# Places of the expert results computed by VectorE for four tiles at once

## The chip, the cores and the metric

The kernel runs on one core of a Trainium2 chip. The metric is device time in microseconds of one launch. TensorE (PE) multiplies, VectorE (DVE), ScalarE (ACT) and GpSimd (POOL) compute, SyncE (SP) issues most transfers, and engines meet only by semaphores.

## The reference

One block of a model on 16 x 512 tokens of width 128, in float32: a modulated layer norm, a linear recurrence (the mixer), then a second modulated layer norm and a mixture of experts, 2 of 8 per token. Cut to what matters here:

```python
logits = xt @ Wr + br
p = softmax(logits)
probs, idx = top_k(p, 2)
probs = probs / probs.sum(axis=-1, keepdims=True)
h = einsum('td,edf->etf', xt, W1) + b1[:, None, :]
h = layernorm(relu(h), g1, be1)
y = einsum('etf,efd->etd', h, W2) + b2[:, None, :]
y = layernorm(relu(y), g2, be2)
gate = (one_hot(idx, 8) * probs[..., None]).sum(axis=1)
out = einsum('te,etd->td', gate, y)
x = x + gb * out
```

## The kernel before

The mixer stage runs over the 16 batches. It writes each token's normalised row twice, into the regions of its two experts in a buffer in device memory (`rows_d`), as a row of ROW = 130 numbers: TOKEN (the number of the result, 2 x token), EXPERT (the token's first expert) and 128 values (H). From about 166 us the expert stage runs over EXPERT_TILES = 135 tiles of 128 such rows; each tile has one expert.

For tile i the work goes so. SyncE loads its rows into `hrow[i % 8]`. TensorE turns them (L1651, step i - 2), ScalarE and VectorE split them into a high and a low part (L821, L1221), TensorE makes the 512 hidden values (L1668 to L1670, step i), ScalarE takes the positive part (L825), VectorE their statistics (L1226, L1484). TensorE turns the hidden values (L1676) and multiplies by W2 (L1686, step i + 4) into one single bank, which VectorE empties in step i + 5 (L1455). There follow ScalarE (L949), statistics (L1474, L1479), a scaling (L1466, step i + 7), and the last scaling and shift, for some tiles on VectorE (L1447), else on ScalarE (L957) and GpSimd (L720). GpSimd stores the 128 result rows with an indirect transfer (L732), whose places are `target[i % 32]`.

These places are the matter here: place = TOKEN + (EXPERT is not the tile's expert). VectorE computes them in `target_of` (L1434 to L1439), one operation per tile at the end of step i:

```python
vec.tensor_scalar(target[i % TARGETS][:], hrow[n][:, EXPERT], tile_e[:, i:i + 1],
                  hrow[n][:, TOKEN], ALU.not_equal, ALU.add).then_inc(target_ready, 1)
```

It waits for the tile's rows and, since `target` has 32 buffers, for the result store 32 tiles back. Who waits for `target_ready`: SyncE in `load_next(i)` (L573 to L580), before it loads rows into the slot of tile i - 8; behind this wait in its queue stand the row load and `load_shifts(i - 6)` (L571), which itself waits until a shift buffer is free. And GpSimd in `store_results` (L722).

The order on each engine is written out by hand: `run_tiles` calls one `expert_step(s)` per step and engine. From step 53 on VectorE also combines the two results of finished tokens (`early_sum`, L1550) in 44 pieces at the end of a step, GpSimd multiplies and adds them (L773, L779), ScalarE scales (L922). In the first 13 steps VectorE makes the second table of tiles between the others (`round2_table`). `tile_e` holds the expert of each tile, on all partitions. GpSimd also writes the last of the mixer's rows (L704), up to step 43. SLOTS is 8.

## Time and profile before

| | |
|---|---|
| median of 3 runs | 505.99 us (504.31 to 506.33) |
| profiled execution | 503.4 us, its span 501.6 us |
| busy over the span | PE 475.5, DVE 452.2, ACT 406.3, POOL 348.3 us |
| operations of VectorE | 2245 |
| transfers | 78.36 MB, mean 156 GB/s |

Busy time counts overlapping operations once. Matmuls are pipelined, so a busy TensorE is not yet at its best rate; the spacing of starts tells more. In a timeline the first number is the start in us from the span's start, the second the duration; the bracket, where there is one, is the idle time before and what ended it. On VectorE an operation may start while the one before it is finishing, so that durations add up to more than the time. "tile" and "step" below count from 0; step s is where TensorE makes the hidden values of tile s.

### The profile page before, as it was taken

How to read it: one execution, taken by the hardware profiler on the slowest of the kernel's cores; microseconds unless marked ns; L12 is line 12 of the kernel's file. 1: busy time of each engine (PE TensorE's matmuls, PEld its weight loads, DVE VectorE, ACT ScalarE, POOL GpSimd, SP SyncE). 2: the span in 40 equal slices, each digit the busy share in tenths (PEclk: the TensorE clock that was granted, in tenths of full speed). 3: DMA queues.
4: the chain of work that ended last, by engine and by line, in shares of the span. 5: the costliest groups of instructions: out<-in, count | busy, mean ns of one | idle time of the engine just before them, and what ended most of it. 6: DMA issues, size and time to landing. Idle time of an engine off the chain costs nothing. (4 is left out here: it accounts for less than half of the span.)

```text
span 501.6 us, 15039 instructions
## 1 busy us (share of the span) xinstructions
PE 475.5 (95%) x3083; PEld 366.6 (73%) x3083; DVE 452.2 (90%) x2245; ACT 406.3 (81%) x1118; POOL 348.3 (69%) x461
## 2 busy tenths in 40 slices
PE   7998999999999899999999999999999999999994
PEld 6454555555567688888888888888888888888851
DVE  6879999998888899899998899999999999999994
ACT  3678898988865777777887888989998889989883
POOL 1003666666767777788888878888887888888871
PEclk9999999999999999999999999999999999999998
DMA  5990511114211578988726986766667667667555
GB/s 165 313 256 18 132 50 48 43 56 106 64 43 56 136 172 163 166 246 205 192 82 160 200 221 137 204 192 185 202 183 178 186 191 207 166 181 212 189 177 167
DMA packets 80364, 78.36 MB, mean 156 GB/s; under 512 B 11433, under 2 KB 73052, under 8 KB 80276
## 3 DMA queue, kind: packets, MB, share of 16 engines
q1 hardware_dynamic: 71860, 60.48, 48.9%
q0 software_dynamic: 8416, 16.93, 9.5%
q8 instruction: 29, 0.48, 0.4%
q14 instruction: 59, 0.48, 0.4%
HBM read 55.20 MB, written 22.62 MB: 155 GB/s over the span
## 5 line engine op out<-in xcount | busy, mean ns | idle before, releaser
L704 POOL DMA_INDIRECT expert_rows<-rows_ring,slot x128 | 123.4, 964 | 93.2 <-issue 74.7
L732 POOL DMA_INDIRECT expert_results<-y,target x119 | 120.4, 1012 | 32.7 <-issue 28.1
L1686 PE MATMUL bank<-W,h2T 128*128 x720 | 96.4, 277 | 1.8 <-DVE wmod L1455 0.9
L1686 PEld LDWEIGHTS bank<-W,h2T 128*128 128x128 f32 x720 | 87.5, 191 | 12.5 <-issue 5.6
L1668 PE MATMUL bank<-W1hi,h3hi 128*128 x135 | 65.5, 485 | 1.3 <-DVE h3lo L1221 1.3
L949 ACT ACTIVATE v<-wmod 128x128 f32<-128x128 f32 x135 | 41.8, 310 | 29.3 <-DVE vg L1466 25.5
L1226 DVE BATCH_NORM_STATS2 stf<-h1T 128x6 f32<-128x512 f32 x90 | 59.2, 658 | 0.0
L814 ACT ACTIVATE n<-X,nm,rs 128x128 f32<-128x128 f32 x128 | 52.7, 488 | 7.1 <-DVE nm L1395 7.1
L961 ACT ACTIVATE sde<-mve,eps 128x2 f32<-128x2 f32 (+1 forms) x138 | 40.6, 295 | 17.9 <-DVE mve L1479 15.6
L1676 PE MATMUL bank<-ident_wr,h1T 128*128 128x128 f32 x360 | 54.4, 274 | 0.2 <-ACT third_rT L829 0.2
L829 ACT ACTIVATE h2T<-bank 128x512 f32<-128x512 f32 x90 | 52.7, 586 | 1.0 <-PE bank L1676 0.9
L1669 PE MATMUL bank<-W1lo,h3hi 128*128 x135 | 53.4, 396 | 0.0
L1670 PE MATMUL bank<-W1hi,h3lo 128*128 x135 | 53.3, 395 | 0.0
L825 ACT ACTIVATE h1T<-bank 128x512 f32<-128x512 f32 x90 | 53.0, 589 | 0.0
L1455 DVE SCALAR_TENSOR_TENSOR wmod<-bank,rse,shifts 128x128 f32<-128x128 f32 x119 | 40.8, 343 | 13.2 <-PE bank L1686 11.9
L1686 PE MATMUL bank<-W,third_rT 128*128 x360 | 48.2, 277 | 1.1 <-DVE wmod L1455 0.9
L1686 PEld LDWEIGHTS bank<-W,third_rT 128*128 128x128 f32 x360 | 43.7, 192 | 6.3 <-issue 2.8
L1466 DVE SCALAR_TENSOR_TENSOR vg<-v,mve,shifts 128x128 f32<-128x128 f32 x119 | 44.7, 376 | 0.0
L1676 PEld LDWEIGHTS bank<-ident_wr,h1T 128*128 128x128 f32 x360 | 41.7, 141 | 1.5 <-issue 0.5
L1221 DVE TENSOR_TENSOR h3lo<-bank,h3hi 128x128 fp32r<-128x128 f32 x135 | 37.9, 281 | 0.5 <-ACT h3hi L821 0.3
L1474 DVE BATCH_NORM_STATS2 sty<-v 128x6 f32<-128x128 f32 x135 | 37.9, 281 | 0.2
L1651 PE MATMUL bank<-ident_wr,hrow 128*128 128x128 f32 x135 | 36.2, 272 | 0.0
(253 smaller groups left out, 1172.0 us busy)
## 6 DMA issues: line engine op xcount, KB each, us to landing
shifts<-expert_shifts SPq DMA_DIRECT2D x119, 192.0 KB
hrow<-expert_rows SPq DMA_DIRECT2D x135, 65.0 KB
xi<-expert_results SPq DMA_DIRECT2D x12, 512.0 KB, 6.0
out_x<-X SPq DMA_DIRECT2D x15, 256.0 KB, 3.9
X<-in_L_attn_x SPq DMA_DIRECT2D x7, 512.0 KB, 7.4
b_ring<-b_two_parts SPq DMA_DIRECT2D x135, 4.0 KB
W1lo<-in_L_ffn_W SPq DMA_DIRECT2D x4, 512.0 KB, 5.9
expert_rows<-rows_ring,slot POOLq DMA_INDIRECT x128
```

The source lines that it names most:

```text
L704: nc.gpsimd.indirect_dma_start(out=rows_d, out_offset=bass.IndirectOffsetOnAxis(ap=slot[q][:, n // TOPK, n % TOPK:n % TOPK + 1], axis=0), ...
L732: nc.gpsimd.indirect_dma_start(out=results_d, out_offset=bass.IndirectOffsetOnAxis(ap=target[i % TARGETS][:], axis=0), in_=y[k], in_offset ...
L814: ins = nc.scalar.activation(dst[:, j:j + 1, :], X[:, bass.ds(b * J + j, 1), :], ACT.Identity, bias=nm_[:, x_tiles + j:x_tiles + j + 1], s ...
L825: nc.scalar.activation(r[i % DEPTH], hidden_bank(i)[:], ACT.Relu).then_inc(r_ready, 1)
L829: nc.scalar.activation(rT[i % DEPTH], turned_bank[:], ACT.Copy).then_inc(rT_ready, 1)
L1226: vec.bn_stats(stf[i % 2][:], r[i % DEPTH]).then_inc(stf_ready, 1)
L1466: vec.scalar_tensor_tensor(wide(vg[p][:]), wide(v[p][:]), mve[p][:, 1, 0:1], wide(shift_rows[ring(s - 7)][:, D:2 * D]), ALU.subtract, ALU. ...
L1668: mm(h, h3hi[i % DEPTH], W1hi[:, bass.ds(e, 1), :], start=False, stop=False)
L1669: mm(h, h3hi[i % DEPTH], W1lo[:, bass.ds(e, 1), :], start=False, stop=False)
L1670: mm(h, h3lo[i % DEPTH], W1hi[:, bass.ds(e, 1), :], start=False, stop=True).then_inc(h_done, 1)
L1676: ins = tr(turned_bank[:, ch * P:(ch + 1) * P], r[i % DEPTH][:, ch * P:(ch + 1) * P], ident[:])
L1686: ins = mm(acc, rT[i % DEPTH][:, ch * P:(ch + 1) * P], W2[:, bass.ds(e * CF + ch, 1), :], start=(ch == 0), stop=(ch == CF - 1))
```

## The change

The eight row slots become one tensor with the slots side by side, and the 32 columns of targets another. In every fourth step (1, 5, 9, ...) VectorE compares the EXPERT column of four slots with four columns of `tile_e` (`other_experts_of`), and after one operation more adds the four TOKEN columns (`targets_of`). The second waits for the first by a new semaphore. Tiles 4k to 4k + 3 are done in step 4k + 1. The semaphore `target_ready` then rises by four at once. The last group has three tiles.

```diff
-        hrow = [sb(f"hrow_{n}", [P, ROW])[:] for n in range(SLOTS)]
+        hrow_ring = sb("hrow_ring", [P, SLOTS, ROW])
+        hrow = [hrow_ring[:, n, :] for n in range(SLOTS)]
...
-        target = [sb(f"target_{n}", [P, 1], I32) for n in range(TARGETS)]
+        targets = sb("targets", [P, TARGETS], I32)
+        target = [targets[:, n:n + 1] for n in range(TARGETS)]
+        TARGETS_AT_ONCE = 4
+        other_expert = sb("other_expert", [P, TARGETS_AT_ONCE])
...
-            def target_of(i, n):
-                dve.wait_ge(hrow_loaded[n], (i + SLOTS - n) * (16 // SLOTS))
+            def other_experts_of(i):
+                count = min(TARGETS_AT_ONCE, EXPERT_TILES - i)
+                for m in range(i, i + count):
+                    dve.wait_ge(hrow_loaded[m % SLOTS], (m + SLOTS - m % SLOTS) * (16 // SLOTS))
+                expert = hrow_ring[:, i % SLOTS:i % SLOTS + count, EXPERT].rearrange("p n o -> p (n o)")
+                vec.tensor_tensor(other_expert[:, 0:count], expert, tile_e[:, i:i + count], ALU.not_equal).then_inc(other_expert_ready, 1)
+
+            def targets_of(i):
+                count = min(TARGETS_AT_ONCE, EXPERT_TILES - i)
+                dve.wait_ge(other_expert_ready, i // TARGETS_AT_ONCE + 1)
                 if i >= TARGETS:
-                    dve.wait_ge(results_stored[(i - TARGETS) % RESULTS], result_count(i - TARGETS))
-                vec.tensor_scalar(target[i % TARGETS][:], hrow[n][:, EXPERT], tile_e[:, i:i + 1],
-                                  hrow[n][:, TOKEN], ALU.not_equal, ALU.add).then_inc(target_ready, 1)
+                    for m in range(i - TARGETS, i - TARGETS + count):
+                        dve.wait_ge(results_stored[m % RESULTS], result_count(m))
+                token = hrow_ring[:, i % SLOTS:i % SLOTS + count, TOKEN].rearrange("p n o -> p (n o)")
+                vec.tensor_tensor(targets[:, i % TARGETS:i % TARGETS + count], other_expert[:, 0:count], token,
+                                  ALU.add).then_inc(target_ready, count)
...
+                if s % TARGETS_AT_ONCE == 1:
+                    other_experts_of(s - 1)
                 if on(s - 6, EXPERT_TILES):
                     ins = value_norm(s, q)
...
-                if on(s, EXPERT_TILES):
-                    target_of(s, n % SLOTS)
+                if s % TARGETS_AT_ONCE == 1:
+                    targets_of(s - 1)
```

On VectorE, at the end of step 61 and in step 62, there stands before (L1479 ends the statistics of the values, L1550 is a combining piece, L1455 empties the value bank):

```order
L1226 BN_STATS stf<-decay 128x6 [waits r_ready]
L1479 BN_AGGR mve<-sty 128x2 [waits sty_ready]
L1438 TENSOR_SCALAR target<-hrow,tile_e 128x1 [waits result_stored5,hrow_loaded5]
L1550 SCALAR_TENSOR_TENSOR n_1<-xi,gate,n_1 128x128 [waits early_y0g_ready]
L1455 SCALAR_TENSOR_TENSOR wmod<-bank,rse,shifts 128x128 [waits rse_ready,shifts_loaded1,y_done]
...
L1226 BN_STATS stf<-h1T 128x6 [waits r_ready]
L1479 BN_AGGR mve<-sty 128x2 [waits sty_ready]
L1438 TENSOR_SCALAR target<-hrow,tile_e 128x1 [waits result_stored6,hrow_loaded6]
L1455 SCALAR_TENSOR_TENSOR wmod<-bank,rse,shifts 128x128 [waits rse_ready,shifts_loaded2,y_done]
```

And in the changed kernel, where the same lines have other numbers (L1494, L1567, L1470; L1444 and L1453 are the pair):

```order
L1231 BN_STATS stf<-decay 128x6 [waits r_ready]
L1444 TENSOR_TENSOR other_expert<-hrow_ring,tile_e 128x4 [waits hrow_loaded6,hrow_loaded7,hrow_loaded5,hrow_loaded4]
L1494 BN_AGGR mve<-sty 128x2 [waits sty_ready]
L1453 TENSOR_TENSOR targets<-other_expert,hrow_ring 128x4 [waits result_stored5,result_stored6,result_stored4,result_stored7,other_expert_ready]
L1567 SCALAR_TENSOR_TENSOR n_1<-xi,gate,n_1 128x128 [waits early_y0g_ready]
L1470 SCALAR_TENSOR_TENSOR wmod<-bank,rse,shifts 128x128 [waits rse_ready,shifts_loaded1,y_done]
...
L1231 BN_STATS stf<-h1T 128x6 [waits r_ready]
L1494 BN_AGGR mve<-sty 128x2 [waits sty_ready]
L1470 SCALAR_TENSOR_TENSOR wmod<-bank,rse,shifts 128x128 [waits rse_ready,shifts_loaded2,y_done]
```

The operation at the end of each step is gone, and one of the pair stands on each side of the value statistics in step 61.

On VectorE in steps 0 to 4, between the making of the second table, there stands before:

```order
L1120 CAST cnt_i<-bank 128x8 [waits count_done,table_ready]
L1438 TENSOR_SCALAR target<-hrow,tile_e 128x1 [waits hrow_loaded0]
L1126 TENSOR_SCALAR cnt<-cnt_i 128x56 [waits counts_ready]
L1438 TENSOR_SCALAR target<-hrow,tile_e 128x1 [waits hrow_loaded1]
L1128 CAST nt_i<-cnt 128x56 [waits table_step]
L1438 TENSOR_SCALAR target<-hrow,tile_e 128x1 [waits hrow_loaded2]
L1484 BN_AGGR mve<-stf 128x2 [waits stf_ready]
L1130 TENSOR_SCALAR nt_i<-nt_i 128x56 [waits table_step]
L1438 TENSOR_SCALAR target<-hrow,tile_e 128x1 [waits hrow_loaded3]
L1463 RECIPROCAL rse<-sde 128x1 [waits sde_ready]
L1221 TENSOR_TENSOR h3lo<-bank,h3hi 128x128 [waits h3hi_ready]
```

and in the changed kernel:

```order
L1125 CAST cnt_i<-bank 128x8 [waits count_done,table_ready]
L1444 TENSOR_TENSOR other_expert<-hrow_ring,tile_e 128x4 [waits hrow_loaded2,hrow_loaded3,hrow_loaded1,hrow_loaded0]
L1131 TENSOR_SCALAR cnt<-cnt_i 128x56 [waits counts_ready]
L1453 TENSOR_TENSOR targets<-other_expert,hrow_ring 128x4 [waits other_expert_ready]
L1133 CAST nt_i<-cnt 128x56 [waits table_step]
L1499 BN_AGGR mve<-stf 128x2 [waits stf_ready]
L1135 TENSOR_SCALAR nt_i<-nt_i 128x56 [waits table_step]
L1478 RECIPROCAL rse<-sde 128x1 [waits sde_ready]
L1226 TENSOR_TENSOR h3lo<-bank,h3hi 128x128 [waits h3hi_ready]
```

Of four operations two are left before the low part of tile 5 (h3lo).

## Rows read from the trace of the kernel before

**Rows 1.** Busy by stretch: length, then PE, PEld, DVE, ACT, POOL (x), clock, DMA

```profile
292.00:468.00 176.00, 175.73 (x1286) 152.34 (x1285) 166.01 (x718) 158.85 (x494) 145.65 (x227) 1.00 0.70 191
```

**Rows 2.** Timeline of TensorE, first hidden matmul of tiles 56, 124, 132: start us, us

```profile
290.81 0.50 PE L1668 MATMUL bank<-W1hi,h3hi 128*128 x1
...
449.80 0.51 PE L1668 MATMUL bank<-W1hi,h3hi 128*128 x1
...
468.18 0.50 PE L1668 MATMUL bank<-W1hi,h3hi 128*128 x1
```

**Rows 3.** Timeline of TensorE: start us, us, operation, [idle before <-releaser]

```profile
168.34 0.49 PE L1668 MATMUL bank<-W1hi,h3hi 128*128 x1 [1.26 <-DVE h3lo L1221]
...
269.47 0.14 PEld L1651 LDWEIGHTS bank<-ident_wr,hrow 128*128 128x128 f32 x1 [0.39 <-DMA hrow<-expert_rows]
...
302.94 0.27 PE L1651 MATMUL bank<-ident_wr,hrow 128*128 128x128 f32 x1
303.05 1.05 PE L1686 MATMUL bank<-W,h2T 128*128 x8
...
305.08 0.27 PE L1651 MATMUL bank<-ident_wr,hrow 128*128 128x128 f32 x1
305.27 1.15 PE L1686 MATMUL bank<-W,h2T 128*128 x8
...
431.80 0.27 PE L1651 MATMUL bank<-ident_wr,hrow 128*128 128x128 f32 x1
432.22 1.15 PE L1686 MATMUL bank<-W,h2T 128*128 x8 [0.15 <-issue]
```

**Rows 4.** Timeline of VectorE, steps 60 to 62 and the end of step 115

```profile
301.01 0.28 DVE L1474 BATCH_NORM_STATS2 sty<-v 128x6 f32<-128x128 f32 x1
...
301.39 0.18 DVE L1479 BATCH_NORM_AGGREGATE mve<-sty 128x2 f32<-128x6 f32 x1
...
302.00 0.35 DVE L1455 SCALAR_TENSOR_TENSOR wmod<-bank,rse,shifts 128x128 f32<-128x128 f32 x1 [0.23 <-PE bank L1686]
...
303.65 0.17 DVE L1479 BATCH_NORM_AGGREGATE mve<-sty 128x2 f32<-128x6 f32 x1
303.73 0.24 DVE L1438 TENSOR_SCALAR target<-hrow,tile_e 128x1 int32<-128x1 f32 x1
303.89 0.86 DVE L1550 SCALAR_TENSOR_TENSOR n<-xi,gate,n 128x128 f32<-128x128 f32 x1
304.68 0.34 DVE L1455 SCALAR_TENSOR_TENSOR wmod<-bank,rse,shifts 128x128 f32<-128x128 f32 x1
...
430.19 0.85 DVE L1550 SCALAR_TENSOR_TENSOR n<-xi,gate,n 128x128 f32<-128x128 f32 x1
```

**Rows 5.** VectorE, single lines: count, then ns min/median/max

```profile
L1438 DVE TENSOR_SCALAR target<-hrow,tile_e x135: 232/242/274, 166.5 to 473.9; 128x1 int32<-128x1 f32 x135
...
L1466 DVE SCALAR_TENSOR_TENSOR vg<-v,mve,shifts x119: 322/332/621, 173.6 to 484.4; 128x128 f32<-128x128 f32 x119
...
L1550 DVE SCALAR_TENSOR_TENSOR n<-xi,gate,n x44: 337/381/948, 287.6 to 485.3; 128x128 f32<-128x128 f32 x44
```

**Rows 6.** Waits: engine, line, releaser: us in total, times, longest us

```profile
ACT v L949 <- DVE vg L1466: 25.5, 51, 1.1
...
SPq L571 <- POOL y L720: 42.8, 34, 9.3
...
SPq L578 <- DVE target L1438: 12.9, 6, 8.3
```

**Rows 7.** Groups of VectorE by line: count | busy us, mean ns | idle before

```profile
L1438 DVE TENSOR_SCALAR target<-hrow,tile_e 128x1 int32<-128x1 f32 x135 | 33.6, 249 | 0.0
...
L1322 DVE TENSOR_TENSOR sq<-rs 128x8 f32<-128x8 f32 (+1 forms) x34 | 5.3, 155 | 0.3
```

**Rows 8.** Timeline of GpSimd

```profile
259.31 0.49 POOL L720 TENSOR_TENSOR y<-wmod,shifts 128x128 f32<-128x128 f32 x1
...
303.72 0.47 POOL L779 TENSOR_TENSOR X<-X,scan 128x128 f32<-128x128 f32 x1
```

1 line of the change is left out of this document (added).

## The prediction, made before the changed kernel ran

> **What bounds the kernel now.** I read the views in this order: busy time by stretch, VectorE's groups by line, the spread of single lines, the timelines of TensorE, VectorE and GpSimd side by side, and last the waits. The change touches only the expert stage, 135 tiles from about 166 us on. In its steady stretch, 292 to 468 us, TensorE shows 175.73 of 176.00 us, VectorE 166.01, ScalarE 158.85 and GpSimd 145.65, at granted clock 1.00 [rows 1]. So TensorE sets the pace and VectorE runs at 94%. How close TensorE is to its own floor is seen in the starts of its first hidden matmul of each fourth tile [rows 2]: tiles 124 to 132 take 468.18 - 449.80 = 18.38 us, 9.19 us for four, and this is the spacing of the undisturbed groups everywhere. From tile 56 (290.81) to tile 132 (468.18) there are 19 groups in 177.37 us; 19 x 9.19 = 174.61, so only 2.8 us of that stretch are above TensorE's floor. No relief of VectorE can give more than that there.
>
> Where those 2.8 us lie is seen at the value matmuls (L1686), which must wait until VectorE has emptied the one value bank (L1455). Normally they start 0.11 us after the row transposition (302.94, 303.05). In step 62 it is 0.19 us (305.08, 305.27), in step 116 0.42 us (431.80, 432.22) [rows 3]. There are four steps in this stretch where VectorE's L1455 starts so late that TensorE must wait for it, of which these are the first and the last. In each of them a combining operation L1550 of 0.80 to 0.86 us stands right before (303.89, 430.19) [rows 4]; its usual time is 0.34 to 0.4, since its spread is 337/381/948 ns [rows 5]. The rest comes through ScalarE, which waits for VectorE's L1466 51 times, 25.5 us in all [rows 6], and then hands TensorE its transposed tile late.
>
> **What the change removes.** 135 operations of 249 ns, 33.6 us [rows 7], become 34 pairs. But the 249 ns overlap the next instruction: from the start of the old operation to the next start is 303.89 - 303.73 = 0.16 us [rows 4]. So in a group of four tiles four times 0.16 = 0.64 us of VectorE's queue go.
>
> **What it adds.** Per group two TENSOR_TENSOR of 128x4. The trace has none; nearest are those of 128x8, 155 ns [rows 7]. An operation of this length lets the next one start 0.08 us later (L1479, 0.17 long, at 303.65, then 303.73) [rows 4]. The second needs the result of the first: the statistics at 301.01 take 0.28 and their dependent starts at 301.39 [rows 4], 0.10 us after the end. So the second may start 0.155 + 0.10 = 0.25 us after the first, and the L1479 put between them (0.08) is hidden in that. The pair costs 0.25 + 0.08 - 0.08 = 0.25 us, all in steps 1, 5, 9 and so on: 0.09 us more than the old operation there, 0.16 us less in each of the other three steps. A group is relieved by 0.39 us; 34 groups by 13 us. As bounds I take 0.16 us for the pair (if nothing of the dependence shows) and, from above, one operation held by GpSimd as below, 0.25 + 0.61.
>
> The additions also wait in a row for four row loads, and then for the pair's own semaphore and four old result stores. The row loads of the group's last tile are asked for two steps earlier than before. They are the same that TensorE needs for its own transposition in about that step, and the result stores are some 20 tiles old, so I cost these waits at nothing; behind them on VectorE's queue stand L1479 (whose result ScalarE waits for) and the next L1455, and if a row load is late both are.
>
> **Held by GpSimd.** The old operation takes 232/242/274 ns in all 135 cases, so nothing ever holds it. Operations with two inputs from the on-chip memory do get held: L1466 goes from 332 to 621 ns and L1550 from 337 to 948 [rows 5], and the 0.86 us one at 303.89 starts 0.17 us after GpSimd's L779 (303.72) [rows 8]. Both new operations are of that kind. In 14 of the 34 groups, as at 303.73, GpSimd starts an addition within 0.02 us of the old operation's start; the first of the pair, put 0.08 us earlier, gets in ahead of it, but the second, due about 0.17 us after the old place, falls into it. In the mild cases (most L1550 at that phase take 0.37 to 0.49) it loses 0.1 us, in the bad ones up to 0.948 - 0.337 = 0.61. I take 0.1 in half of the groups, since 381 is L1550's median. The relief is then 0.34 us a group.
>
> The Trainium skill, SBUF — State Buffer, section Who interferes with whom, says that a VectorE instruction with two SBUF inputs contends with a GpSimd instruction that reads SBUF, and that the later one is blocked for the whole of the other. By it every one of those seconds would lose what is left of GpSimd's 0.47 us. The rows agree that such operations are held, but show most of them held for less than that.
>
> **What of the relief reaches the end.** TensorE is at its floor in most groups, so there the relief becomes idle time of VectorE. Of the four late steps from 292 us on, three follow a step that loses an old operation and is not the pair's, and the wait before them shrinks by at most 0.16 us each: -0.48. Step 62 follows step 61, where the pair stands: +0.1. Through ScalarE, in the twelve or so steps (92 to 104) in which VectorE hardly idles, I put another -0.3, two removed operations. Sum: **-0.7 us**.
>
> Before 292 us there is more to gain by VectorE: TensorE waits 1.26 us for it at the start of the stage (168.34) [rows 3], and two removed operations lie ahead of this and the next such wait, worth about 0.3 us; a few stalls between 183 and 232 us give another 0.5. But I count nothing for either. GpSimd works off a backlog at its own pace there; SyncE waits up to 9.3 us, longest of its 34 waits, until GpSimd has added a shift [rows 6], which happens with the addition at 259.31 [rows 8], and the loads issued behind it are so late that TensorE waits 0.39 us for a row tile at 269.47 [rows 3]. Whoever arrives there 0.8 us earlier waits 0.8 us longer. What is late next is that load.
>
> **Moved past SyncE.** SyncE reloads a row slot only when its target is made. It waits for that 6 times, 12.9 us, of which 8.3 is the first [rows 6], ending as the stage starts. The first tile of each group is released one step (2.3 us) later than before, the last two earlier. From tile 47 on SyncE asks for tile i more than 1 us after step i-7 has ended, so the later release is not felt; in tiles 30 to 46 it is, but there the row is asked for 10 us before it is needed. Cost: nothing; without that cover up to 2.3 us per group.
>
> The profiled execution is 503.4 us (span 501.6), 2.6 below the median of 505.99; the sum gives 502.7 for it, and 505.3 for the median.
>
> **Rivals.**
> 1. *Every stall but the loads' is VectorE's lateness and goes.* Then the 2.8 us from 292 us on and 0.3 us at the start are won: 505.99 - 3.1 = 502.9. For it: the median run is 2.6 us longer than the profiled one, and may have more such stalls. Against: some stalls of about 0.3 us stand where VectorE was in time.
> 2. *GpSimd wins the port (slower).* The second of the pair, which also waits for the first, is caught by two back-to-back additions of GpSimd, as L1550 was at 303.89. In the 14 groups where the phases meet, step 1 becomes 0.25 - 0.16 + 0.61 = 0.7 us longer. TensorE has 0.45 us before it needs L1455, as its value matmuls normally start 1.05 us after it (302.00, 303.05) and where they wait 0.59 (304.68, 305.27) [rows 3, 4]. It decides when the hold exceeds about 0.36 us. Then ScalarE's share is late too, whose spare is small, and the whole 0.7 us is lost: 14 x 0.7 = 9.8, that is 515.8; if only what exceeds 0.45, 14 x 0.25 = 3.5: 509.5. I take 509.5. By the page named above this case would be more frequent than the rows make it.
> 3. *Nothing reaches the end*, or a row load that now comes in bursts of four makes good the 0.7: 506 to 507.
> 4. That the pair doesn't do what it says has no room: the order has 34 of each and none of the old.
>
> **How the numbers follow.** My case (505.3) 0.55, rival 1 (502.9) 0.18, rival 3 (506.5) 0.17, rival 2 (509.5) 0.1. A measurement of this kernel can tell about 0.5%, 2.5 us, from no change; the three runs before lie 2 us apart. Faster by over 0.5% is rival 1 and a little of mine: 0.2. Slower: rival 2, 0.1. The rest, 0.7, is same. The range takes in rivals 1 and 3 with a margin for the spread of the runs: 502.6 to 507.8.
>
> **What would show it.** VectorE's busy time falls by about 13 us or less (busy is counted once where operations overlap), the pair's operations take 0.15 to 0.2 us with a few above 0.4, the group from tile 124 to 128 still takes 9.19 us, the stretch from tile 56 to 132 becomes 176.7 us, and the row load near tile 49 still makes TensorE wait, rather longer. It is wrong if groups that took 9.19 us take more (rival 2), if tile 49's wait vanishes and the gain before 269 us is kept, or if the 2.8 us shrink below 1.

## The result

The changed kernel takes 506.96 us (median of 13 runs, 505.65 to 509.98), the kernel before, run beside it, 504.31 us (13 runs, 502.91 to 511.03). The ratio is 1.0051, 95% interval 1.0033 to 1.0070: slower by about 2.6 us, where the prediction had it faster by 0.7. The profiled execution is 507.31 us, its span 505.5 (503.4 and 501.6 before). VectorE's work did shrink: it is busy 441.6 us in place of 452.2.

### The profile page after: what moved, and what is told of

The parts are those of the page before. It is cut to its first block, busy times and chain, and to the rows that moved or that the text cites. A ratio compares the mean times of both kernels' runs of the same rounds, so it can differ in the third digit from the quotient of the medians.

```text
span 505.5 us, 15021 instructions
## 1 busy us (share of the span) xinstructions
PE 478.8 (95%) x3083; PEld 368.2 (73%) x3083; DVE 441.6 (87%) x2178; ACT 406.5 (80%) x1118; POOL 348.6 (69%) x461
## 4 chain that ended last, share of the span: by engine, by line
POOL 29%; issue 20%; POOLq 2%; DVE 1%; DMA 1%; DVEq 0%; ACT 0%; SPq 0%
POOL expert_results L737 17%; POOL y L725 4%; POOL X L784 3%; POOL scan L778 2%; POOL expert_rows L709 2%; POOLq L736 1%; DMA W<-expert_results 1%; POOLq L737 1%; DMA expert_results<-y,targets 1%; POOL xi L725 0%; POOLq L68 0%; POOLq L724 0%; DVE W L1574 0%; POOLq L735 0%; DVE W L1605 0%
## 5 line engine op out<-in xcount | busy, mean ns | idle before, releaser
L737 POOL DMA_INDIRECT expert_results<-y,targets x119 | 120.1, 1009 | 33.2 <-issue 30.6
L1703 PE MATMUL bank<-W,h2T 128*128 x720 | 97.2, 278 | 2.1 <-DVE wmod L1470 1.4
L1703 PEld LDWEIGHTS bank<-W,h2T 128*128 128x128 f32 x720 | 88.3, 193 | 13.2 <-issue 6.1
L954 ACT ACTIVATE v<-wmod 128x128 f32<-128x128 f32 x135 | 41.8, 310 | 31.1 <-DVE vg L1481 25.7
L1685 PE MATMUL bank<-W1hi,h3hi 128*128 x135 | 65.4, 484 | 1.1 <-DVE h3lo L1226 1.1
L1470 DVE SCALAR_TENSOR_TENSOR wmod<-bank,rse,shifts 128x128 f32<-128x128 f32 x119 | 40.9, 344 | 24.5 <-PE bank L1703 21.2
L1693 PE MATMUL bank<-ident_wr,h1T 128*128 128x128 f32 x360 | 55.3, 276 | 0.4 <-ACT third_rT L834 0.2
L834 ACT ACTIVATE h2T<-bank 128x512 f32<-128x512 f32 x90 | 52.9, 587 | 0.9 <-PE bank L1693 0.8
L1686 PE MATMUL bank<-W1lo,h3hi 128*128 x135 | 53.2, 394 | 0.0
L1703 PE MATMUL bank<-W,third_rT 128*128 x360 | 48.2, 277 | 1.0 <-DVE wmod L1470 0.9
L1703 PEld LDWEIGHTS bank<-W,third_rT 128*128 128x128 f32 x360 | 43.7, 191 | 6.3 <-issue 2.8
L1693 PEld LDWEIGHTS bank<-ident_wr,h1T 128*128 128x128 f32 x360 | 41.0, 142 | 2.9 <-issue 0.9
L1481 DVE SCALAR_TENSOR_TENSOR vg<-v,mve,shifts 128x128 f32<-128x128 f32 x119 | 42.7, 359 | 0.0
L1668 PE MATMUL bank<-ident_wr,hrow_ring 128*128 128x128 f32 x135 | 36.3, 273 | 0.0
```

The source lines that it names most:

```text
L737: nc.gpsimd.indirect_dma_start(out=results_d, out_offset=bass.IndirectOffsetOnAxis(ap=target[i % TARGETS][:], axis=0), in_=y[k], in_offset ...
L834: nc.scalar.activation(rT[i % DEPTH], turned_bank[:], ACT.Copy).then_inc(rT_ready, 1)
L1481: vec.scalar_tensor_tensor(wide(vg[p][:]), wide(v[p][:]), mve[p][:, 1, 0:1], wide(shift_rows[ring(s - 7)][:, D:2 * D]), ALU.subtract, ALU. ...
L1685: mm(h, h3hi[i % DEPTH], W1hi[:, bass.ds(e, 1), :], start=False, stop=False)
L1686: mm(h, h3hi[i % DEPTH], W1lo[:, bass.ds(e, 1), :], start=False, stop=False)
L1693: ins = tr(turned_bank[:, ch * P:(ch + 1) * P], r[i % DEPTH][:, ch * P:(ch + 1) * P], ident[:])
```

## The profile after

The lines of the changed kernel have moved: L1438 is now the pair L1444 and L1453, L1455 is L1470, L1466 is L1481, L1550 is L1567, TensorE's L1668, L1676 and L1686 are L1685, L1693 and L1703, ScalarE's L829 and L949 are L834 and L954, GpSimd's L720 is L725.

Busy time by stretch in the changed kernel, in the columns of [rows 1]:

```profile
292.00:468.00 176.00, 175.29 (x1265) 150.63 (x1265) 156.86 (x671) 156.63 (x484) 143.58 (x223) 1.00 0.69 186
```

VectorE is 9.15 us less busy than in [rows 1], and TensorE gets through less: 1265 recorded matmul instructions in place of 1286. The timeline of TensorE in the changed kernel, first hidden matmul of tiles 56, 124 to 128 and 132, which answers to [rows 2]:

```profile
291.76 0.50 PE L1685 MATMUL bank<-W1hi,h3hi 128*128 x1
...
452.99 0.50 PE L1685 MATMUL bank<-W1hi,h3hi 128*128 x1
...
455.15 0.48 PE L1685 MATMUL bank<-W1hi,h3hi 128*128 x1
...
457.29 0.48 PE L1685 MATMUL bank<-W1hi,h3hi 128*128 x1
...
459.53 0.48 PE L1685 MATMUL bank<-W1hi,h3hi 128*128 x1
...
462.34 0.50 PE L1685 MATMUL bank<-W1hi,h3hi 128*128 x1
...
471.71 0.50 PE L1685 MATMUL bank<-W1hi,h3hi 128*128 x1
```

The group from tile 124 to 128 takes 462.34 - 452.99 = 9.35 us, the next 9.37; before they took 9.2. From tile 56 to 132 it is 179.95 us in place of 177.37, that is 2.6 us, as much as the medians differ. The two profiled executions differ by 3.9 us: 0.9 lie ahead of tile 8 (the clock, see the last section), 0.1 from there to tile 56, these 2.6, and 0.4 behind tile 132. In the kernel before, the starts of tiles 130, 131 and 132 are:

```profile
463.30 0.48 PE L1668 MATMUL bank<-W1hi,h3hi 128*128 x1
...
465.44 0.48 PE L1668 MATMUL bank<-W1hi,h3hi 128*128 x1
```

with 468.18 in [rows 2]: 2.14 and 2.74 us. At the same places of the changed kernel's group (126, 127, 128) it is 2.24 and 2.81. So the group loses 0.10 us in the step after the pair's and 0.07 us in the next.

What VectorE does just before that is seen in its timeline. The kernel before, step 129, from one L1455 to the next:

```profile
461.00 0.35 DVE L1455 SCALAR_TENSOR_TENSOR wmod<-bank,rse,shifts 128x128 f32<-128x128 f32 x1 [0.24 <-PE bank L1686]
...
462.73 0.24 DVE L1438 TENSOR_SCALAR target<-hrow,tile_e 128x1 int32<-128x1 f32 x1
462.89 0.34 DVE L1550 SCALAR_TENSOR_TENSOR n<-xi,gate,n 128x128 f32<-128x128 f32 x1
463.15 0.34 DVE L1455 SCALAR_TENSOR_TENSOR wmod<-bank,rse,shifts 128x128 f32<-128x128 f32 x1
```

and GpSimd there:

```profile
463.00 0.56 POOL L720 TENSOR_TENSOR y<-wmod,shifts 128x128 f32<-128x128 f32 x1
```

The changed kernel, the same place of a group (step 125), VectorE:

```profile
454.99 0.35 DVE L1470 SCALAR_TENSOR_TENSOR wmod<-bank,rse,shifts 128x128 f32<-128x128 f32 x1 [0.88 <-PE bank L1703]
...
456.64 0.15 DVE L1444 TENSOR_TENSOR other_expert<-hrow_ring,tile_e 128x4 f32<-128x4 f32 x1
456.70 0.18 DVE L1494 BATCH_NORM_AGGREGATE mve<-sty 128x2 f32<-128x6 f32 x1
456.88 0.17 DVE L1453 TENSOR_TENSOR targets<-other_expert,hrow_ring 128x4 int32<-128x4 f32 x1
456.96 0.57 DVE L1567 SCALAR_TENSOR_TENSOR n<-xi,gate,n 128x128 f32<-128x128 f32 x1
457.45 0.34 DVE L1470 SCALAR_TENSOR_TENSOR wmod<-bank,rse,shifts 128x128 f32<-128x128 f32 x1
```

and GpSimd:

```profile
456.92 0.46 POOL L725 TENSOR_TENSOR y<-win,shifts 128x128 f32<-128x128 f32 x1 [0.28 <-ACT win L962]
```

Three things are to be seen. The pair costs what was forecast: the combining operation starts 1.97 us after the step's L1470 in place of 1.89. But it now starts 0.04 us behind GpSimd's addition (456.92), where it used to start 0.11 us ahead of it (463.00), and it takes 0.57 us in place of 0.34; before, it was GpSimd's addition that took 0.56 in place of 0.46. So the next L1470 comes 2.46 us after the last, in place of 2.15. And the relief of the other three steps lies in the bracket of the first row: VectorE idles 0.88 us there, until TensorE has filled the value bank. The waits say the same. Kernel before, then after:

```profile
DVE wmod L1455 <- PE bank L1686: 12.7, 49, 0.7
```

```profile
DVE wmod L1470 <- PE bank L1703: 22.1, 32, 1.1
```

VectorE waits for TensorE 9.4 us more, in fewer and longer pieces.

The rest of the way is on ScalarE and TensorE. The changed kernel, ScalarE (its relu of the values, then its copy of the turned tile), then TensorE (value matmuls, transposition of the hidden tile):

```profile
458.20 0.31 ACT L954 ACTIVATE v<-wmod 128x128 f32<-128x128 f32 x1 [0.34 <-DVE vg L1481]
458.42 0.58 ACT L834 ACTIVATE h2T<-bank 128x512 f32<-128x512 f32 x1
```

```profile
458.18 1.08 PE L1703 MATMUL bank<-W,third_rT 128*128 x8
459.14 0.63 PE L1693 MATMUL bank<-ident_wr,h1T 128*128 128x128 f32 x4
```

The copy ends at 458.42 + 0.58 = 459.00, and the transposition, which needs its buffer, starts 0.14 us later. That 0.14 is the least distance between the two in any of the traces. In the kernel before, at the same place:

```profile
464.13 0.58 ACT L829 ACTIVATE h2T<-bank 128x512 f32<-128x512 f32 x1
```

```profile
464.19 1.06 PE L1686 MATMUL bank<-W,h2T 128*128 x8
465.08 0.60 PE L1676 MATMUL bank<-ident_wr,decay 128*128 128x128 f32 x4
```

it is 465.08 - 464.71 = 0.37 us. So ScalarE's copy, which stands behind the relu, which waits for VectorE's L1481, has a spare of 0.37 - 0.14 = 0.23 us. VectorE is late by 2.46 - 2.15 = 0.31. The value matmuls themselves take that without loss: they start 0.73 us after L1470 in place of 1.04.

Of the 19 steps 1, 5, 9 ... between 292 and 468 us, 13 have a combining operation. It takes over 0.45 us in 11 of them in the changed kernel and in 1 of them before. Group by group against the kernel before, these 11 lose 1.8 us. The other two with a combining operation (steps 61 and 77) lose 0.7, and there the pair itself is late. In step 61 its second operation is the one that is held; GpSimd's additions start at 304.74 and 305.21 there:

```profile
305.01 0.67 DVE L1453 TENSOR_TENSOR targets<-other_expert,hrow_ring 128x4 int32<-128x4 f32 x1
```

In step 77 it starts 0.35 us late. Of the 6 groups without a combining operation, four have the next L1470 2.13 to 2.14 us after the last. In steps 89 and 101 the pair's second operation takes 0.45 and 0.72 us, the next L1470 comes 2.36 and 2.83 us after the last, and these two groups lose 0.2 and 0.55 us; as the other four gain nearly as much, the six together lose only 0.1. In the second pair of profiles (below) the held groups lose 0.5 us, those of steps 61, 77 and 117, in which the pair is late, 1.1, and the six 0.3. So the split between the two kinds of hold changes with the execution. The second operation of the pair over the whole kernel (min/median/max in ns):

```profile
L1453 DVE TENSOR_TENSOR targets<-other_expert,hrow_ring x34: 153/166/724, 166.8 to 475.6; 128x4 int32<-128x4 f32 x33, 128x3 int32<-128x3 f32 x1
```

## The experiments

In all tables and texts "held" is a combining operation of over 0.45 us in one of those 13 steps, and "56 to 132" the time from the first hidden matmul of tile 56 to that of tile 132, both read from the timeline of each kernel as above. "Quiet" groups are those that take 9.18 to 9.21 us in the kernel before. The stretch comes from one profiled execution: two profiles of the kernel before and the one of layout give 177.4, 177.8 and 178.4 us, so differences below about 1 us say little.

| kernel | ratio to before (95%) | 56 to 132 | held, of 13 |
|---|---|---|---|
| before (profile shown ahead) | | 177.4 us | 1 |
| changed | 1.0051 (1.0033 to 1.0070) | 180.0 | 11 |
| changed, again | 1.0049 (1.0026 to 1.0073) | 179.7 | 10 |
| layout | 0.9986 (0.9967 to 1.0005) | 178.4 | 1 |
| burst | 1.0111 (1.0080 to 1.0141) | 181.6 | 0 |
| pair0 | 0.9984 (0.9965 to 1.0002) | 178.2 | 7 |
| pair_after_sum | 1.0029 (1.0018 to 1.0041) | 179.2 | 1 |
| twos | 1.0045 (1.0030 to 1.0061) | 178.8 | 8 |
| split | 1.0040 (1.0025 to 1.0056) | 177.9 | 6 |
| pair3 | 1.0158 (1.0141 to 1.0175) | 180.8 | 10 |
| delay | 1.0048 (1.0026 to 1.0070) | 179.9 | 9 |
| delay_after | 1.0011 (0.9990 to 1.0032) | 178.5 | 1 |
| turned2 | 1.0029 (1.0006 to 1.0053) | 180.2 | 11 |
| pair0_turned | 0.9965 (0.9943 to 0.9986) | 177.1 | 10 |
| before, again | 0.9994 (0.9970 to 1.0018) | 177.8 | 1 |
| turned_only | 0.9962 (0.9943 to 0.9981) | 175.8 | 5 |
| split2 | 1.0005 (0.9983 to 1.0027) | 177.9 | 3 |
| pair0_turned, again | 0.9964 (0.9942 to 0.9986) | 176.9 | 10 |

### First set: layout, lump, place

**The changed kernel again.** No edit.

> The changed kernel once more, beside the others of this set. It tells whether the 1.2 GHz stretch of TensorE at 169 to 172 us, which only the changed kernel's trace showed and which cost it about 0.9 us at tile 8, belongs to the change. If the loss is a lump on VectorE in every fourth step (my theory), the ratio is again 1.005, groups of four tiles from 292 us on take 9.35 us instead of 9.19, whatever the clock does at 169 us. If the loss were mostly that stretch of low clock (rival), a profile without it would show a time of about 505 us and quiet groups of 9.19.

Measured 1.0049, and the quiet groups at the end are 9.36 us each. The stretch at 1.2 GHz is there again; what it is worth is settled by the kernel before again, below.

**Layout.**

```diff
-        hrow = [sb(f"hrow_{n}", [P, ROW])[:] for n in range(SLOTS)]
+        hrow_ring = sb("hrow_ring", [P, SLOTS, ROW])
+        hrow = [hrow_ring[:, n, :] for n in range(SLOTS)]
...
-        target = [sb(f"target_{n}", [P, 1], I32) for n in range(TARGETS)]
+        targets = sb("targets", [P, TARGETS], I32)
+        target = [targets[:, n:n + 1] for n in range(TARGETS)]
```

> The kernel before with the row slots in one ring tensor and the targets in one tensor, still one operation per tile; nothing else is changed. Theory (the lump in steps 1, 5, 9 ...): same time as before, ratio 1.000 within 0.001, groups of 9.19 us. Rival (where the slots and targets lie in the on-chip memory makes the loads, the transposition or VectorE's readers slower): ratio 1.005 as the whole change.

Measured 0.9986, held 1 of 13. The ring and the common tensor are not the cause.

**Burst.** Four old operations together, in the steps where the change has its pair.

```diff
-                if on(s, EXPERT_TILES):
-                    target_of(s, n % SLOTS)
+                if s % 4 == 1:
+                    for i in range(s - 1, min(s + 3, EXPERT_TILES)):
+                        target_of(i, i % SLOTS)
```

> As layout, but the four old operations of a group stand together in steps 1, 5, 9 ..., where the change has its pair. They have one on-chip tensor input and two per-partition scalars each and were never held by GpSimd. The lump is 0.64 us instead of 0.25. Theory (a lump in one step makes VectorE late there, what is freed in the other three steps becomes idle time): slower than the changed kernel, since 0.48 us are added to the step instead of 0.09 to 0.2; TensorE has about 0.45 us to spare, so at least 0.2 us a group and up to 0.5, 34 groups: ratio 1.01 to 1.03. Rival (the loss comes from the two-input operations held by GpSimd, or from the wait of the second for the first): no slower than before beyond 1.002. Rival (the loss comes from the release of row slots in bursts, which SyncE waits for): ratio 1.005 as the whole change, since the releases are the same.

Measured 1.0111, the quiet groups 9.60 us. So a lump of work in that step can cost time by itself: its +0.48 us cost a group 0.41 us. No combining operation is held here, as it starts 2.43 us after L1457, when GpSimd's addition is over. The row slots are released as in the changed kernel and the loss is more than twice as large, so the release alone doesn't set it.

**The pair one step earlier.**

```diff
-                if s % TARGETS_AT_ONCE == 1:
-                    other_experts_of(s - 1)
+                if s % TARGETS_AT_ONCE == 0:
+                    other_experts_of(s)
...
-                if s % TARGETS_AT_ONCE == 1:
-                    targets_of(s - 1)
+                if s % TARGETS_AT_ONCE == 0:
+                    targets_of(s)
```

> The changed kernel with the pair one step earlier, in steps 0, 4, 8 ..., for the tiles s to s+3 instead of s-1 to s+2. In the changed kernel VectorE idles 0.88 us before L1470 at the end of such a step. Theory: the pair fits into that idle time, step 1 is freed of it, TensorE's groups are 9.19 us again: time of before or up to 1 us below, ratio 0.998 to 1.001. Rival (the form of the operations, their hold by GpSimd or their dependence costs, wherever they stand): ratio 1.005 again. Rival (releases of row slots in bursts): 1.005 again or more, as three rows must now be there earlier.

Measured 0.9984: the loss is gone. The pair's second operation is held there far more often than in the changed kernel (over 0.4 us in 12 of 34 cases in place of 4). VectorE's timeline at the end of step 128:

```profile
462.40 0.59 DVE L1453 TENSOR_TENSOR targets<-other_expert,hrow_ring 128x4 int32<-128x4 f32 x1
463.22 0.35 DVE L1470 SCALAR_TENSOR_TENSOR wmod<-bank,rse,shifts 128x128 f32<-128x128 f32 x1 [0.22 <-PE bank L1703]
```

It takes 0.59 us and costs nothing, since L1470 still waits 0.22 us for TensorE. The combining operation of step 1 is held in 7 of 13 steps too, but it starts 0.17 us earlier than before the change (1.72 us after L1470), and the next L1470 still comes only 2.11 to 2.14 us after the last in six of the seven. In five groups VectorE waits 0.78 to 1.32 us for a row load. Neither the kind of the operations nor this early wait for four rows is the cause; the place is.

### Second set: which part of step 1

**The second operation behind the combining one.**

```diff
-                if s % TARGETS_AT_ONCE == 1:
-                    targets_of(s - 1)
                 for b, j in pieces_at(s - 1):
                     early_sum(b, j)
+                if s % TARGETS_AT_ONCE == 1:
+                    targets_of(s - 1)
```

> The changed kernel, but in steps 1, 5, 9 ... the second operation of the pair comes after the combining operation L1567 instead of before it. In the changed kernel L1567 starts at 456.96, 0.04 us after GpSimd's addition at 456.92, and takes 0.57 us, where in the kernel before it took 0.34. If this hold is what makes VectorE late (part of my theory), L1567 is 0.34 us again in quiet groups, and TensorE's groups shrink from 9.35 to 9.20 us: ratio to before 1.000 to 1.002. If the length of the pair itself is enough (rival), the groups stay at 9.3 or more: ratio 1.005. If the second operation is now the one that is held, for 0.2 us or more, the same 1.005.

Measured 1.0029, groups of 9.33 us. VectorE and GpSimd in step 125 of this kernel:

```profile
455.37 0.32 DVE L1567 SCALAR_TENSOR_TENSOR n<-xi,gate,n 128x128 f32<-128x128 f32 x1
455.60 0.44 DVE L1453 TENSOR_TENSOR targets<-other_expert,hrow_ring 128x4 int32<-128x4 f32 x1
455.97 0.34 DVE L1470 SCALAR_TENSOR_TENSOR wmod<-bank,rse,shifts 128x128 f32<-128x128 f32 x1
```

```profile
455.49 0.53 POOL L725 TENSOR_TENSOR y<-win,shifts 128x128 f32<-128x128 f32 x1 [0.29 <-ACT win L962]
```

The combining operation is ahead of the addition again and takes 0.32 us, and the small one behind it is the one held, 0.44 in place of 0.17. The next L1470 comes 2.40 us after the last, 0.25 later than before the change. Half of my first expectation was wrong: taking the hold from L1567 only hands it on to the next operation with two inputs.

**Two at a time.** Layout, with two old operations in each odd step.

```diff
-                if on(s, EXPERT_TILES):
-                    target_of(s, n % SLOTS)
+                if s % 2 == 1:
+                    for i in range(s - 1, min(s + 1, EXPERT_TILES)):
+                        target_of(i, i % SLOTS)
+                elif s == EXPERT_TILES - 1:
+                    target_of(s, s % SLOTS)
```

> Old operations, two together in each odd step, none in the even steps (ring and targets as in the layout run). A lump of +0.16 us with operations that GpSimd never holds. In the burst run +0.48 us cost TensorE 0.40 us a group. If TensorE has no spare at all in such a step (theory), +0.16 costs 0.1 to 0.16 us in steps 1, 5, 9 ... and nearly as much in steps 3, 7, 11 ...: groups of 9.3 to 9.5 us, ratio 1.004 to 1.009. If a step has 0.1 us or more to spare (rival), the quiet groups stay at 9.19 to 9.22: ratio 0.999 to 1.001, and the changed kernel's loss needs the hold of L1567 or the wait of the second operation besides.

Measured 1.0045, at the lower end of what was expected. But the reason is not the 0.16 us alone. The combining operation starts 2.07 us after L1457, where GpSimd's addition starts too (mostly from 0.03 us later to 0.15 earlier), and is held in 8 of 13 steps. This run has both cases side by side. In steps 65, 69, 121 and 125 it is not held, the next L1457 comes 2.32 or 2.33 us after the last, and the groups take 9.23 to 9.25 us. (The fifth that is not held, step 129, has 2.32 and a group of 9.52: TensorE's weight load starts 0.43 us late at 464.78, released by nothing that the profile shows, as in the second profile of the kernel before at 464.71, 0.33 us.) The eight held ones have 2.45 to 2.81 us and groups of 9.41 to 9.77. So 0.18 us of lateness cost a group about 0.05 us, and the hold on top of it the rest. In five of the 6 steps without a combining operation the next start is 2.13 or 2.14 us after the last.

The twos profile is no guide to the ratio: it took 504.42 us, the fastest of its six runs, whose median is 506.25.

**The pair split over steps 0 and 1.**

```diff
-                if s % TARGETS_AT_ONCE == 1:
-                    other_experts_of(s - 1)
+                if s % TARGETS_AT_ONCE == 0:
+                    other_experts_of(s)
```

> The changed kernel with the first operation of the pair in steps 0, 4, 8 ... and the second where it was, in steps 1, 5, 9 .... The second no longer waits for the first, and step 1 holds one short operation (0.08 us) in place of the old one (0.16 us): no lump. Theory: quiet groups 9.19, ratio 0.997 to 1.001, as the run with the pair one step earlier. Rival (the hold by GpSimd of whatever has two inputs in step 1 is the cost): groups over 9.25 in those where GpSimd's addition starts just before, ratio 1.002 to 1.005.

Measured 1.0040, though step 1 has less work than in the kernel before. Held 6 of 13. Its step 121, VectorE and GpSimd:

```profile
446.00 0.36 DVE L1453 TENSOR_TENSOR targets<-other_expert,hrow_ring 128x4 int32<-128x4 f32 x1
446.28 0.61 DVE L1567 SCALAR_TENSOR_TENSOR n<-xi,gate,n 128x128 f32<-128x128 f32 x1
446.81 0.34 DVE L1470 SCALAR_TENSOR_TENSOR wmod<-bank,rse,shifts 128x128 f32<-128x128 f32 x1
```

```profile
445.86 0.47 POOL L784 TENSOR_TENSOR X<-X,scan 128x128 f32<-128x128 f32 x1
446.27 0.46 POOL L725 TENSOR_TENSOR y<-wmod,shifts 128x128 f32<-128x128 f32 x1
```

L1453 starts 0.14 us into GpSimd's addition of the early output (445.86) and takes 0.36; that puts L1567 0.01 us behind the next addition, and it takes 0.61. The old operation at this place, with one such input, was never held. In the other seven steps of the 13, in five of them with L1567 at 1.78 us, ahead of an addition at 1.93, it takes 0.34 to 0.35 us. So step 1 can be late with no lump in it. But the 1.0040 is not the price of these holds: from tile 56 to 132 the profile has 177.9 us, 0.1 to 0.5 more than the two of the kernel before. Its loss lies ahead, 116.4 us from tile 8 to 56 in place of 114.7 and 113.9, with a wait of 0.89 us for a row load at 264.15 among it; VectorE waits 2.80 us for rows just then, in the pair's first operation, which stands a step earlier here. No combining operation runs before step 53. What exactly this run pays there is open.

**The pair in steps 3, 7, 11 ...**

```diff
-                if s % TARGETS_AT_ONCE == 1:
-                    other_experts_of(s - 1)
+                if s % TARGETS_AT_ONCE == 3 or s == EXPERT_TILES - 1:
+                    other_experts_of(s - s % TARGETS_AT_ONCE)
...
-                if s % TARGETS_AT_ONCE == 1:
-                    targets_of(s - 1)
+                if s % TARGETS_AT_ONCE == 3 or s == EXPERT_TILES - 1:
+                    targets_of(s - s % TARGETS_AT_ONCE)
```

> The changed kernel with the pair in steps 3, 7, 11 ... for the tiles s-3 to s; the row slots of a group are released two steps later than in the changed kernel. Theory: only the step before the long idle time of VectorE (step 0, where TensorE also multiplies the biases of four tiles) has room for a lump; step 3 hasn't, so groups of 9.25 to 9.4 us: ratio 1.003 to 1.006, and more if a row load comes too late. Rival (what counts is the kinds of operation or step 1 alone, where ScalarE hands the turned tile over late): groups 9.19, ratio 0.998 to 1.001.

Measured 1.0158, far more than expected, 8 us. The profile accounts for a part of it: 180.8 us from tile 56 to 132, and L1453 has a median of 277 ns and a maximum of 880. The rest of the 8 us is not explained.

### Third set: push or length

**Delay ahead of the combining operation.** Layout, and

```diff
                     target_of(s, n % SLOTS)
+                if s % 4 == 1:
+                    vec.reciprocal(unused[:], eps[:])
```

> The layout run (old operations, one a tile) with one extra reciprocal of 128x1 on VectorE, about 0.07 us, in steps 1, 5, 9 ... right before the combining operation. It stands for the 0.08 us by which the pair pushes that operation: 1.89 us after the step's L1455 in the kernel before, 1.97 after the pair, while GpSimd's addition starts at 1.93 to 2.00. Theory (the push lets GpSimd win, the combining operation then takes 0.57 instead of 0.34 us and TensorE waits for ScalarE): groups go from 9.19 to 9.3 or 9.4 in those where the addition starts before, ratio to before 1.002 to 1.006. Rival (only the work in the step counts, and 0.07 us is within ScalarE's spare of 0.37 - 0.14 = 0.23 us): groups stay at 9.19, ratio 0.998 to 1.001.

**Delay behind it.** The same two lines, after early_sum.

> The same extra reciprocal of 128x1 in steps 1, 5, 9 ..., but behind the combining operation. The work in the step is the same as in the delay run, and the combining operation still starts at 1.89 us, ahead of GpSimd's addition. Theory (order against GpSimd decides, not length): the next L1455 is 0 to 0.08 us later, within the spare, groups stay at 9.19 to 9.21, ratio 0.998 to 1.001. Rival (length decides): the same loss as in the delay run.

Measured 1.0048 and 1.0011, with intervals against the kernel before that just meet (1.0026 and 1.0032); run beside each other, 12 runs each, the medians are 507.94 and 506.01 us. 56 to 132 is 179.9 and 178.5 us; held 9 and 1. The same amount of work in the same step costs as much as the whole change in the one place, and next to nothing in the other. VectorE in step 117, first with the delay ahead, then behind:

```profile
437.23 0.24 DVE L1441 TENSOR_SCALAR targets<-hrow_ring,tile_e 128x1 int32<-128x1 f32 x1
437.39 0.16 DVE L1540 RECIPROCAL unused<-eps 128x1 f32<-128x1 f32 x1
437.46 0.66 DVE L1555 SCALAR_TENSOR_TENSOR n<-xi,gate,n 128x128 f32<-128x128 f32 x1
```

```profile
436.55 0.34 DVE L1555 SCALAR_TENSOR_TENSOR n<-xi,gate,n 128x128 f32<-128x128 f32 x1
436.81 0.16 DVE L1542 RECIPROCAL unused<-eps 128x1 f32<-128x1 f32 x1
436.88 0.33 DVE L1458 SCALAR_TENSOR_TENSOR wmod<-bank,rse,shifts 128x128 f32<-128x128 f32 x1
```

and GpSimd's addition in each:

```profile
437.50 0.47 POOL L723 TENSOR_TENSOR y<-win,shifts 128x128 f32<-128x128 f32 x1
```

```profile
436.64 0.56 POOL L723 TENSOR_TENSOR y<-win,shifts 128x128 f32<-128x128 f32 x1
```

An 0.07 us push, with operations of the kernel before and not one of the change, gives the change's loss. The delay kernel also shows it within itself: in steps 65, 113, 121 and 129 its combining operation starts 0.08 to 0.13 us ahead of the addition and takes 0.33 or 0.34 us, the next L1458 comes 2.21 or 2.22 us after the last, and the groups take 9.19 to 9.21 us. In the nine held steps it is 2.46 to 2.81, and the groups take 9.38 to 9.75. This is the experiment that carries the verdict.

**ScalarE's copy first in steps 2, 6, 10 ...** The changed kernel, and

```diff
-                turned_first = s >= EXPERT_TILES or last_of_group
+                turned_first = s >= EXPERT_TILES or last_of_group or s % TOGETHER == 2
```

> The changed kernel, with ScalarE copying the turned tile ahead of its relu of the values in steps 2, 6, 10 ... too, as it already does in steps 0, 4, 8 .... TensorE's transposition then no longer waits, in those steps, for VectorE's L1470 and L1481. Theory (VectorE's 0.3 us of lateness reaches TensorE through ScalarE's copy, whose spare is 0.23 us): the wait of 0.08 to 0.1 us in step 2 goes and groups shrink from 9.36 to 9.2 or 9.27 (a part may come back in step 3): ratio 1.001 to 1.003. Rival (TensorE waits for the value bank or for loads): no change, 1.005.

Measured 1.0029, but with an interval that reaches from 1.0006 to 1.0053, and 180.2 us from tile 56 to 132: inconclusive on time. The trace says more. The copy's end stands, as a median, 0.71 us ahead of the transposition in those steps, never less than 0.24, in place of 0.14. With that TensorE's loss there is gone: from the first hidden matmul of tile 130 to that of 131 it takes 2.15 us, where the changed kernel takes 2.24 and the kernel before 2.14. But quiet groups stay at 9.35 to 9.39 us. What step 2 no longer loses, step 3 does, with 2.90 us in place of 2.82: VectorE's L1470 follows without idle time (1.8 to 1.9 us after the one before in the quiet groups) and is still late there, and the copy's end is at 0.14 or 0.15 us again. So ScalarE's copy is shown to be the way by which step 2 is late; moving it in one step doesn't bring the time back.

**The pair in step 0 and the copy first everywhere.** pair0, and

```diff
-                turned_first = s >= EXPERT_TILES or last_of_group
+                turned_first = True
```

> The pair in steps 0, 4, 8 ... and ScalarE's copy of the turned tile ahead of its relu in every step: an attempt at a version faster than both. Theory: TensorE's small waits for ScalarE behind the value matmuls (28 above 0.03 us, 3.6 us in all in the run with the pair at step 0) mostly go, if the later relu does not make VectorE's statistics late: ratio 0.991 to 0.998. Rival: the relu is now 0.2 us later in each step, the statistics and ScalarE's root with it, and it is as it was or slower: 0.998 to 1.005.

Measured 0.9965, and 0.9964 in the repeat below: faster than both kernels, 503.61 us. It is so although the combining operation is held in 10 of 13 steps. The copy's end is now 0.5 to 0.9 us (medians of steps 3, 2 and 1) ahead of the transposition, and 14 of the 19 groups are at 9.17 to 9.25 us, held or not.

### Fourth set: what was still open

**The kernel before again.**

> The kernel before once more. Ratio 1.000. If the 1.2 GHz stretch near 169 us belongs to single executions (theory: it has been in the profiles of five kernels with different edits and absent from six others), its profile may or may not have it, and the groups from tile 56 on are 9.19 us in the quiet ones, 177 to 178.5 us from tile 56 to 132. If it belongs to the changed code (rival), it is absent here.

Measured 0.9994. Its profile has the stretch at 1.2 GHz, which the first profile of the same code has not: it belongs to single executions (by then 7 of 14 profiles had it, not the five and six that the expectation counts). 56 to 132 is 177.8 us, so the change's loss there is 2.6 us by the first pair of profiles and 179.66 - 177.79 = 1.9 by the second.

**ScalarE's order alone.** Layout with `turned_first = True`.

> The layout run (old operations, one a tile) with ScalarE's copy of the turned tile ahead of its relu in every step. If the gain of the faster version comes from ScalarE's order, this has it all: ratio 0.995 to 0.998. If it comes from the pair's place (which alone measured 0.9984, within its interval of no change), this stays at 0.999 to 1.001. I expect most of it from ScalarE's order: 0.997.

Measured 0.9962, 502.6 us: the whole gain of the faster version is ScalarE's order, with or without the pair. From tile 56 to 132 it needs 175.8 us, 1.2 us above 19 times the 9.19 of a group. The busy times by stretch:

```profile
292.00:468.00 176.00, 176.00 (x1295) 153.24 (x1294) 164.53 (x724) 157.41 (x496) 145.96 (x230) 1.00 0.69 192
```

**The second operation in step 2.**

```diff
+                if s % TARGETS_AT_ONCE == 2:
+                    targets_of(s - 2)
                 if on(s - 6, EXPERT_TILES):
                     ins = value_norm(s, q)
...
-                if s % TARGETS_AT_ONCE == 1:
-                    targets_of(s - 1)
```

> The changed kernel with the pair's first operation in steps 1, 5, 9 ... as it was and the second in steps 2, 6, 10 ... ahead of the value norm. Step 1 then holds 0.08 us where the kernel before has 0.16, so the combining operation starts at 1.81 us after L1470, ahead of GpSimd's addition at 1.93, as before. Theory: no hold, quiet groups 9.19 to 9.25, ratio 0.998 to 1.002. Rival (an operation on four tiles costs wherever it is outside step 0, or step 2's combining operation is now the one that is held): 1.003 to 1.005.

Measured 1.0005, held 3 of 13. VectorE in step 129:

```profile
463.89 0.15 DVE L1444 TENSOR_TENSOR other_expert<-hrow_ring,tile_e 128x4 f32<-128x4 f32 x1
463.96 0.18 DVE L1494 BATCH_NORM_AGGREGATE mve<-sty 128x2 f32<-128x6 f32 x1
464.05 0.32 DVE L1567 SCALAR_TENSOR_TENSOR n<-xi,gate,n 128x128 f32<-128x128 f32 x1
464.39 0.35 DVE L1470 SCALAR_TENSOR_TENSOR wmod<-bank,rse,shifts 128x128 f32<-128x128 f32 x1
```

The combining operation starts 0.13 us ahead of GpSimd's addition (464.18) and the loss is gone, with the pair still outside step 0.

**The faster version again.** No edit.

> The faster version once more: the pair in steps 0, 4, 8 ..., ScalarE's copy ahead of its relu in every step. Ratio 0.996 to 0.997, as in its first run (0.9965), and 0 to 0.002 below ScalarE's order alone.

Measured 0.9964, not below ScalarE's order alone.

## Why the prediction was wrong

**What bounds the kernel: right.** TensorE sets the pace, 9.19 us a group at best, and the relief of VectorE is worth nothing where TensorE is at its floor.

**What the change removes and adds: right in size.** Forecast, the pair costs 0.25 us in place of 0.16 in its step; measured, where the pair itself isn't held, what follows it starts 0.08 us later. Busy time falls by 10.6 us, within "13 or less". The median of L1453 is 166 ns, with a few above 400.

**Held by GpSimd: here the sum failed.** The step put the hold mostly on the wrong operation and at the wrong price. It watched the pair's second operation and gave it "0.1 in half of the groups". That operation takes its 0.17 us in 16 of the 19 groups from tile 56 on, and 0.45, 0.67 and 0.72 in the other three, near the bad case of the forecast. The count behind it, "in 14 of the 34 groups" an addition within 0.02 us of the old operation's start, doesn't come out of the trace: there it is one, at 303.73, while in ten groups the addition starts 0.14 to 0.16 us ahead of the old operation. What was exposed besides was the operation queued behind the pair: the combining one, which in the kernel before starts 0.04 to 0.11 us ahead of GpSimd's addition in the quiet steps. I had its row of the bad case (303.89, taken 0.17 us behind an addition) and did not look how narrowly the good cases had escaped. The push of 0.08 us, costed at 0.08 us, costs 0.31: its own 0.08 and about 0.23 by the hold, in 11 of the 13 steps that have a combining operation. The delay runs show this second hold with the change's own operations absent, and it alone gives a loss as large as the whole change's.

**What of the relief reaches the end: wrong.** The -0.48 and -0.3 us did not come. L1470 of every step 1, 5, 9 ... waits for TensorE's bank, so VectorE starts each group anew there; what is saved in the three steps before it is idle time (mean 0.81 us before that L1470 in the changed kernel, 0.27 before) and can't be carried over to the step with the pair. The step after the pair is then late by the full 0.31.

**Rival 2 had the way, with a wrong threshold.** It let the hold decide above 0.36 us, from the 0.45 us that the value matmuls can wait. They do take the lateness. The nearer limit is the one that rival named and left unpriced: ScalarE's copy behind the relu, with 0.23 us. VectorE's 0.31 exceeds that by 0.08, TensorE loses 0.10 in that step and 0.07 more in the next, 0.17 a group. Group by group the eleven with a held combining operation lose 1.8 us in the first pair of profiles, the two in which the pair itself is late 0.7, and the rest 0.1: together the 2.6 us; in the second pair of profiles it is 0.5, 1.1 and 0.3, together 1.9. The rival's 3.5 was too much since it lost 0.25 in each of 14.

**The waits past SyncE and for four rows: right at nothing,** as far as the profiles show: pair0 has them a step earlier and no loss. The changed kernel does have waits of VectorE's L1470 for a load of shifts, 0.59 and 1.07 us at 198.63 and 209.13 in one profile and 1.30 at 293.77 in the other, the like of which neither profile of the kernel before has; the group with the 1.30 is 0.08 us longer than the same group of the first profile. But "the row load near tile 49 still makes TensorE wait" was wrong: the changed kernel's first profile has no such wait and its second 0.19 us (269.34), and the kernel before, again, has its only one at 284.04 (0.47 us). It belongs to an execution, not to the kernel, and so did the reason for which I counted the gains ahead of 292 us at nothing. They did not come either, by the profiles: from tile 8 to 56 the changed kernel takes 114.8 and 114.5 us, the kernel before 114.7 and 113.9.

**The number.** The measured 506.96 us is inside the forecast range, and rival 3 had 506 to 507 for it. That is luck: the forecast started from 505.99 us, the median of three runs, and the kernel before measures 504.31 here. Against that the change costs 2.6 us, which neither the forecast nor rival 3 had.

**What stays open:** why the pair in steps 3, 7, 11 ... costs 8 us, what split pays ahead of tile 56, and why TensorE loses 0.10 us where VectorE's excess is 0.08.

## What to carry to other kernels

Before moving an operation by a tenth of a microsecond, look at what stands behind it on its queue and how far that is from the other engine's start that it must beat: a narrow escape in every steady step is a cliff, and a median duration doesn't show it. Work saved ahead of a point where the engine waits anyway can't pay for work added behind it. For each wait of the bounding engine take the spare of every path that leads into it, by the distance from the last result to the start that uses it; here the second path had half the spare of the first, and reordering two operations on it was worth more than the change.

## What the runs showed of the hardware

**Who wins between VectorE and GpSimd is decided within a few hundredths of a microsecond.** An operation of VectorE with two inputs from the on-chip memory that starts 0.09 to 0.13 us ahead of GpSimd's addition takes its 0.32 to 0.34 us, and the addition 0.51 to 0.56 in place of 0.46 (462.89 against 463.00, 436.55 against 436.64). One that starts 0.04 or 0.01 us behind takes 0.57 or 0.61, and the addition its 0.46. In between it goes either way. In the delay run it is held although its record starts 0.04 us ahead (437.46 against 437.50, 0.66 us); in the kernel before, steps 57 and 109, the same 0.04 us are enough (0.34 us, the addition 0.61 and 0.62). In the twos run, 0.01 us ahead, it takes 0.34 or 0.35 us in steps 65 and 69 and 0.61 or 0.62 in steps 77 and 81.

What is left of a longer addition need not hold it. In the kernel before, GpSimd's addition at 462.58 takes 0.46 us, and VectorE's operation at 462.89, with two inputs and 0.31 us behind it, still takes 0.34.

The Trainium skill, SBUF — State Buffer, section Who interferes with whom, says that a VectorE instruction with two SBUF inputs contends with a GpSimd instruction that reads SBUF, and, of VectorE's two-port modes, that whoever issues first gets the shared pair for the whole instruction while the other fully blocks. The order deciding agrees with these rows. The length agrees less: at 456.96 the addition had 0.42 us to go, and the hold was 0.57 - 0.34 = 0.23.

**TensorE's clock near 169 us.** At the start of the expert stage TensorE idles 0.98 to 1.63 us in every profile (1.26 before 168.34, [rows 3]). In half of the 18 profiles the granted clock then goes to 0.50 (1.2 GHz) for about three microseconds, in the other half it stays at 1.00, and the same code does both. Busy time by stretch, the kernel before, then the same kernel again:

```profile
169.00:170.00 1.00, 0.56 (x4) 0.20 (x3) 1.00 (x8) 0.64 (x3) 0.70 (x2) 1.00 0.65 152
```

```profile
169.00:170.00 1.00, 1.00 (x4) 0.39 (x3) 1.00 (x8) 0.64 (x3) 0.69 (x2) 0.50 0.67 151
```

Tile 8 starts at 176.09 in the first and 177.14 in the second: 1.05 us, more than the whole effect forecast for the change, and it comes and goes with the single execution. A comparison of two single profiles would have put it on the change.
